# Two binary convolutions: packing in the weights instead of the activations, half of a pair at a time

## The reference

```python
def _L0_conv_ref(x, ...):           # called with _gn(x)
    xr = jnp.tile(x, (1, 4, 1, 1))                                    # 4 parallel groups
    out = bconv3x3(xr, w1, groups=4)                                  # sign(x), sign(w): 256 channels
    out = relu(batchnorm(out, bn1...))
    out = bconv3x3(out, w2, groups=4)                                 # sign(relu(.)) is 0 or 1
    out = batchnorm(out, bn2...) * repeat(lambdas, 64)
    out = out.reshape(B, 4, 64, H, W).sum(axis=1)
    return relu(out + identity)
def _L1_conv_ref(x, masks, conv_w, ...):  # called with _gn(x)
    m = resize(masks, 28 x 28); mid = x * m
    atten = sigmoid(conv7x7(concat([mean_c(mid), max_c(mid), m])))
    out = mid * atten
    rn = instance_norm(out) * in_gamma + in_beta
    return relu(5 * rn)
x = x + _L0_conv_ref(_gn(x), ...)
x = x + _L1_conv_ref(_gn(x), ...)
```

## Time and profile before

| | us |
|---|---|
| median of 3 runs (300.37 to 301.81) | 300.83 |
| profiled execution, its own time | 298.91 |
| span of that execution, first to last instruction | 297.1 |
| PE busy | 238.0 (80%) |
| DVE busy | 216.5 (73%) |
| POOL busy | 182.9 (62%) |
| ACT busy | 159.2 (54%) |
| granted TensorE clock, mean over the span | 0.918 of full |

### The profile page before, as it was taken

One profiled execution on the slowest core, in us unless ns is written; L12 is line 12 of the kernel. 1 busy time (PEld: TensorE's weight loads), 2 busy tenths in 40 slices (PEclk: granted clock), 3 DMA queues, 4 the chain that ended last, 5 costly groups with the idle time before them and its releaser, 6 DMA issues.

```text
span 297.1 us, 6991 instructions
## 1 busy us (share of the span) xinstructions
PE 238.0 (80%) x2742; PEld 152.4 (51%) x2742; DVE 216.5 (73%) x523; ACT 159.2 (54%) x191; POOL 182.9 (62%) x215
## 2 busy tenths in 40 slices
PE   8293998698998989897988798979879896866850
PEld 4262754355565556554654565456536454643640
DVE  3349642759776797989888887998696869656362
ACT  2432251275757657575758575756665774444121
POOL 2300410224534577798787969896979697967762
PEclk9668777689999999999999999999999999988775
DMA  7990000713015321632173115122512331141014
GB/s 199 307 310 14 0 2 2 182 48 110 3 57 160 114 55 58 183 97 103 58 209 113 61 61 160 57 56 85 135 54 56 119 103 57 57 160 57 0 56 162
DMA packets 11947, 28.86 MB, mean 97 GB/s; under 512 B 2286, under 2 KB 3566, under 8 KB 11758
## 3 DMA queue, kind: packets, MB, share of 16 engines
q1 hardware_dynamic: 11481, 28.13, 30.5%
q10 hardware_dynamic: 432, 0.29, 0.4%
HBM read 21.79 MB, written 6.61 MB: 96 GB/s over the span
## 4 chain that ended last, share of the span: by engine, by line
PE 56%; DVE 23%; issue 11%; DMA 3%; ACT 3%; POOL 3%; SPq 1%; POOLq 0%; DVEq 0%; ACTq 0%
PE big L901 16%; PE big L887 13%; PE big L918 10%; DVE gate L619 5%; PE small L947 5%; PE small L936 4%; DVE RD L634 4%; DVE bnst L563 4%; DMA X<-in_x 3%; DVE S L625 2%; PE small L991 2%; ACT word L471 2%; DVE red L658 2%; PE small L863 1%; POOL o L359 1%
## 5 line engine op out<-in xcount | busy, mean ns | idle before, releaser
L901 PE MATMUL big<-S,w2t 64*64 64x392 f16 x1152 | 57.3, 353 | 7.4 <-DVE S L625 7.4
L936 PE MATMUL small<-cs,o 128*112 128x130 f32 x224 | 35.1, 303 | 26.6 <-POOL o L359 19.3
L887 PE MATMUL big<-E,w1t 64*128 64x392 f16 x576 | 55.2, 334 | 0.0
L634 DVE TENSOR_SCALAR RD<-word 128x784 f16<-128x784 uint16 x32 | 33.1, 1035 | 22.2 <-ACT word L471 22.2
L901 PEld LDWEIGHTS big<-S,w2t 64*64 64x64 f16 x1152 | 33.9, 113 | 26.2 <-DVE S L625 5.1
L936 PEld LDWEIGHTS small<-cs,o 128*112 128x112 f32 x224 | 28.8, 190 | 35.7 <-POOL o L359 25.2
L359 POOL TENSOR_TENSOR o<-o,mask_b 128x784 f32<-128x784 f32 x16 | 35.6, 2226 | 15.4 <-ACT o L491 15.4
L471 ACT ACTIVATE word<-big 128x784 int32<-128x784 f32 x32 | 26.1, 815 | 27.1 <-PE big L901 27.1
L377 POOL TENSOR_TENSOR X<-X,acc 128x784 f32<-128x784 f32 x15 | 29.3, 1957 | 13.9 <-ACT acc L485 13.9
L918 PE MATMUL big<-RD,wa 128*64 128x392 f16 x384 | 36.1, 339 | 0.6 <-DVE RD L634 0.6
L887 PEld LDWEIGHTS big<-E,w1t 64*128 64x128 f16 x576 | 25.7, 95 | 21.0 <-issue 4.5
(11 more groups left out here) (118 smaller groups left out, 336.1 us busy)
## 6 DMA issues: line engine op xcount, KB each, us to landing
X<-in_x SPq DMA_DIRECT2D x16, 392.0 KB, 6.0
mask_b<-mask_rows SPq DMA_DIRECT2D x32, 196.0 KB, 3.5
out<-o SPq DMA_DIRECT2D x16, 392.0 KB, 2.4
att_b<-attention_rows SPq DMA_DIRECT2D x28, 196.0 KB, 3.7
o<-in_w SPq DMA_DIRECT2D x3, 576.0 KB, 9.1
o<-in_masks SPq DMA_DIRECT2D x1, 512.0 KB, 10.6
cs<-in_cst SPq DMA_DIRECT2D x1, 385.0 KB, 11.9
o<-in_sel SPq DMA_DIRECT2D x1, 343.0 KB
```

The lines of the kernel that those rows point to most:

```text
L634: dve.tensor_scalar(RD[:, t % 2, hh, 1, :], low2[:, hh, :], LIFT, 1.0 / UNIT, ALU.subtract, ALU.mult).then_inc(split, 1)
L887: mm = pe.matmul(acc[:, LOW + HALF * hh:LOW + HALF * (hh + 1)], w1t[64 * hh:64 * hh + 64, s, q * P:(q + 1) * P], window(RH * hh, s // 3, s ...
L901: mm = pe.matmul(acc[64 * q:64 * q + 64, LOW + HALF * r:LOW + HALF * (r + 1)], w2t[64 * r:64 * r + 64, s, 64 * q:64 * q + 64], window(RH * ...
L936: mm = pe.matmul(small[1 - n % 2][0:CP, at:at + P + 2], o[:, t, CP * j:CP * (j + 1)], cs[:, K_ID:K_ID + P + 2], start=True, stop=True)
```

## The change

What it does, by parts:

- **First convolution.** The two images of a pair are no longer joined. `sign_x` writes signs straight into `E`, image i on its own 64 partitions. Instead two channel blocks (output channels 0 to 127 and 128 to 255) are packed into one weight, 2046 times one sign plus the other. `join` and `pack_signs` go; the join matrix is used once, on the weights (`join_weights`). `conv1(t, step)` now makes 15 rows of each image in step 0 and 13 in step 1 (from the top for image 0, from the bottom for image 1), all 256 channels in words of 128 partitions.
- **Words.** `words1` and `words2` write the 32-bit words in place over the sums in PSUM. The tiles `word1`, `word2` and `gate0` are gone.
- **Gates.** ACT makes the gate of the high half by a steep sigmoid of the 16-bit half in PSUM (`high_gates`), DVE that of the low half by one comparison (`low_gates`), which waits for the former. Both write their own tile in `S`.
- **Second convolution.** Its weights are packed too (1024 times one half of the output channels plus the other), so its tiles are 64 rows by 32 columns, 8 of them, and there are 72 matmuls per half instead of 36. `high_sums` (ACT) and `low_sums` (DVE, waits for it) read the word in PSUM.
- **Mix.** Tiles of 64 by 32, four at a time, 24 matmuls per half instead of 12. Its weights are made by one DVE instruction instead of 12 on POOL.
- **PSUM.** `c1`, `c2` and `y` have one buffer each (two banks), and each half of a pair waits for the half before it to be read.
- **Order.** All four loops run over k = 1 to 22 and hold the end as well. `finish_block(k-1)` stands last in DVE's round but for `last_sum`, `relu_block` first in ACT's. The second block's steps are one round later than before. No `keep_clock` stands in the end.
- **Preparations.** w1 arrives as 128 partitions by 1152 values on ACT's DMA queue; the matrices of the 7 by 7 convolution are made on the host and loaded (`band_in`, 441 KB) instead of being made by 28 matmuls. Masks, thresholds and mix scales are as before with 6 instead of 4 columns. `repeat_picks` goes from ACT to POOL. Pairs 14 and 15 no longer send their attention through DRAM.

POOL's loop first, then ACT, DVE and PE; lines of "..." stand where lines are left out:

```diff
+            for k in range(1, STEPS):
+                if k in TERMS_AT:
+                    power1(batch(k + 1))
+                add_x(k - 2)
+                if (k - 5) % 2:
+                    attend(k - 5)
+                    scale3(k - 6)
+                    power2(k - 2)
+                else:
+                    scale3(k - 6)
+                    power2(k - 2)
+                    attend(k - 5)
+                last_sum(k - 6)
+                make_u(k - 2)
                 mask_column(k - 2)
...
+                act.activation(inside(E[:, t % 2, :]), X[:, t, :].rearrange("p (h w) -> p h w", w=W), ACT.Sign,
+                               bias=nm1[:, t:t + 1]).then_inc(signed, 1)
+
+            def words1(t, hh):
+                if has(t):
+                    act.wait_ge(conv1_done, 2 * t + hh + 1)
+                    act.activation(first_sums(hh).bitcast(I32), first_sums(hh), ACT.Copy, bias=WORD / 2,
+                                   scale=WORD / IMG).then_inc(worded1, 1)
+
+            def high_gates(t, hh):
+                if has(t):
...
+                    act.wait_ge(worded1, 2 * t + hh + 1)
+                    wait(act, conv2_done, 2 * t - 2)
+                    act.activation(gate_rows(t, hh, 0), by_rows(high_of(first_sums(hh))), ACT.Sigmoid,
+                                   bias=thr_high[:, :], scale=STEEP).then_inc(gated_high, 1)
...
+                    act.wait_ge(conv2_done, 2 * t + hh + 1)
+                    act.activation(second_sums().bitcast(I32), second_sums(), ACT.Copy, bias=LIFT,
+                                   scale=2.0 * UNIT).then_inc(worded2, 1)
+
+            def high_sums(t, hh):
+                if has(t):
+                    act.wait_ge(worded2, 2 * t + hh + 1)
+                    wait(act, y_done, 2 * t + hh - 1)
+                    act.activation(RD[:, hh, 0, :], high_of(second_sums()), ACT.Copy).then_inc(high2, 1)
...
+            act.dma_start(w1f, w1).then_inc(w1_in, 16)
...
+            for m in range(3):
+                act.activation(w1s[:, 3 * m:3 * m + 3, :].rearrange("p k o -> p (k o)"),
+                               w1f[:, 3 * m * P:3 * (m + 1) * P], ACT.Sign).then_inc(w1_signs, 1)
+            act.wait_ge(w1_joined, 3)
+            act.activation(w1t[:, 6:9, :].rearrange("p k o -> p (k o)"), y[:, 0:3 * P], ACT.Copy).then_inc(w1_ready, 1)
...
+            for k in range(1, STEPS):
+                relu_block(k - 2)
+                words1(k, 0)
+                high_gates(k, 0)
                 words2(k - 1, 1)
-                high_half(k - 1, 1)
+                high_sums(k - 1, 1)
                 sign_x(k + 1)
-                words1(k, 0)
+                last_relu(k - 6)
+                words1(k, 1)
+                high_gates(k, 1)
                 normalise2(k - 2)
-                words1(k, 1)
-                relu_block(k - 1)
-                pack_signs(k + 1)
-                last_relu(k - 5)
                 words2(k, 0)
-                high_half(k, 0)
-                sigmoid(k - 2)
```

```diff
+            def low_gates(t, hh):
...
+                    dve.wait_ge(gated_high, 2 * t + hh + 1)
+                    dve.tensor_scalar(gate_rows(t, hh, 1), by_rows(low_of(first_sums(hh))), thr_low[:, :], None,
+                                      ALU.is_gt).then_inc(gated_low, 1)
+
+            def low_sums(t, hh):
+                if has(t):
+                    dve.wait_ge(high2, 2 * t + hh + 1)
+                    dve.tensor_scalar(RD[:, hh, 1, :], low_of(second_sums()), LIFT, 1.0 / UNIT,
+                                      ALU.subtract, ALU.mult).then_inc(low2, 1)
...
+            def scale_weights(m):
+                dve.wait_ge(w1_signs, m + 2)
+                dve.tensor_tensor(w1p[:, 3 * m:3 * m + 3, :], w1s[:, 3 * m:3 * m + 3, :],
+                                  scale_s[:, :].unsqueeze(1).to_broadcast([P, 3, P]), ALU.mult).then_inc(w1_scaled, 1)
+
+            def keep_weights(m):
+                dve.wait_ge(w1_joined, m + 1)
+                dve.tensor_copy(w1t[:, 3 * m:3 * m + 3, :].rearrange("p k o -> p (k o)"),
+                                c2[:, 512 * m:512 * m + 3 * P]).then_inc(w1_ready, 1)
...
+            scales()
+            for m in range(3):
+                scale_weights(m)
+            for m in range(2):
+                keep_weights(m)
+            thresholds()
             stats_x(1)
-            sign_weights()
+            low_gates(0, 0)
             terms1(1)
+            flip_weights()
...
+            for k in range(1, STEPS):
+                if k in TERMS_AT:
...
+                attend_last(k - 5)
+                stats_o(k - 6)
...
+                low_gates(k, 0)
+                if k in TERMS_AT:
+                    make_bias1(batch(k + 1))
+                if k == 1:
+                    keep_mask_rows()
+                stats_x1(k - 2)
+                low_sums(k - 1, 1)
+                terms2(k - 2)
+                reduce_chunks(k - 3, 0)
+                reduce_chunks(k - 3, 1)
+                low_gates(k, 1)
+                reduce_chunks(k - 3, 2)
+                low_sums(k, 0)
+                finish_block(k - 1)
+                last_sum(k - 6)
```

```diff
-                wait(pe, sigm, t // 2)
+                wait(pe, y_added, t + 1)
...
+            def conv1(t, hh):
...
+                wait(pe, gated_low, 2 * t + hh)
+                wait(pe, gated_high, 2 * t + hh)
+                n = ROWS[hh] * W
                 for s in range(KS):
-                    for hh in range(2):
-                        mm = pe.matmul(acc[:, LOW + HALF * hh:LOW + HALF * (hh + 1)],
-                                       w1t[64 * hh:64 * hh + 64, s, q * P:(q + 1) * P],
-                                       window(RH * hh, s // 3, s % 3, E[64 * hh:64 * hh + 64, t % 2, :]),
+                    for i in range(2):
+                        mm = pe.matmul(c1[:, 512 - n * (1 - i):512 + n * i], w1t[64 * i:64 * i + 64, s, :],
+                                       window(START[i][hh], ROWS[hh], s, E[64 * i:64 * i + 64, t % 2, :]),
                                        start=(s == 0), stop=(s == KS - 1))
                 mm.then_inc(conv1_done, 1)
...
+                pe.wait_ge(gated_low, 2 * t + hh + 1)
+                pe.wait_ge(gated_high, 2 * t + hh + 1)
+                wait(pe, low2, 2 * t + hh)
+                wait(pe, high2, 2 * t + hh)
+                for s in range(KS):
                     for r in range(2):
-                        for q in range(2):
-                            mm = pe.matmul(acc[64 * q:64 * q + 64, LOW + HALF * r:LOW + HALF * (r + 1)],
-                                           w2t[64 * r:64 * r + 64, s, 64 * q:64 * q + 64],
-                                           window(RH * hh, s // 3, s % 3, S2[64 * r:64 * r + 64, t % 2, q, :]),
-                                           start=(s == 0), stop=(s == 8))
+                        for i in range(2):
+                            for q in range(2):
+                                at = Q32 * (2 * i + q)
+                                mm = pe.matmul(c2[at:at + Q32, LOW + HALF * r:LOW + HALF * (r + 1)],
+                                               w2t[64 * r:64 * r + 64, s, q, :],
+                                               window(RH * half_of(i, hh), RH, s, S[64 * r:64 * r + 64, t % 2, i, q, :]),
+                                               start=(s == 0), stop=(s == KS - 1))
...
+            for k in range(1, STEPS):
                 conv1(k, 0)
-                if k == 2:
+                conv2(k - 1, 1)
+                if k == 1:
+                    turn_mask()
+                mix(k - 1, 0)
+                group_2(k - 2)
+                if k == 3:
                     pe.wait_ge(mask_rows, 2)
-                group_2(k - 2)
+                turn(k - 3, 0)
+                turn(k - 3, 1)
                 conv1(k, 1)
-                if k == 1:
-                    pe.wait_ge(band_ready, 1)
-                    turn_mask()
-                    pe.wait_ge(var1, 3)
-                    band_matrices(1)
-                mix(k - 1, 0)
+                turn(k - 3, 2)
+                conv2(k, 0)
+                attention(k - 3)
                 mix(k - 1, 1)
-                join(k + 1)
-                if k == 2:
-                    pe.wait_ge(band_ready, 2)
-                for n in range(3):
-                    turn(k - 2, n)
-                conv2(k, 0)
```

More of the change, by code:

```diff
@@ L954, in keep_clock @@
                 for _ in range(n):
-                    pe.matmul(big[2][:, LOW:512], warm[:, 0:P], warm[:, :], start=True, stop=True)
+                    pe.matmul(small[0][:, 0:HALF], warm[:, 0:P], warm[:, :], start=True, stop=True)
             def spread_attention(t):
+                if not has(t) or t < POOL_ATTENDS:
+                    return
                 if t == POOL_ATTENDS:
```

618 lines of the change are left out of this document (244 added, 374 removed).

## The result

The changed kernel takes 333.99 us (median of 4 runs, 326.93 to 336.71) against 300.6 (300.13 to 301.81), ratio 1.0949 [1.0802, 1.1097]. The profile is of an execution of 336.22 us. A second set of runs of the same kernel gave 326.2 (322.80 to 329.27), ratio 1.077 [1.0682, 1.0858]. Forecast were 317.6 and a range to 334, whose upper end the first median just touches. Before spreads over 1.7 us, the changed kernel over 9.8 in the first set and 6.5 in the second, which will need a reason.

The account below looks back on a forecast made before the run. No engine was full, so waits between engines bound the round; the change would make a loop of 15.1 us. Rounds +15.1, start -4.8, end +5.0 and +1.5 gave +16.8 us: 317.6 us, with 304 to 334 holding 8 in 10.

Parts of the forecast that it names:

- start: Up to the end of `finish_block(1)`: conv1(0,0) at about 11, conv1(1,0) at 32 to 34, end at 63.0; -4.8 us.
- 13 rounds: From `finish_block(1)` to `finish_block(14)`: 13 x 15.1 + 2.1 = 198.4 against 183.3; +15.1 us.
- end: After `finish_block(14)`: last pairs go one behind the other, 51.0 against 46.0, +5.0 us, plus 1.5 for a slower clock.
- The loop: Path through the engines' ordered lists, one pair per turn: 14.7 us, 15.1 with some 14 handovers of 0.03 to 0.04.
- ACT 2.73 (2.82 forecast): First step of a round, on ACT: `relu_block`, `words1(k,0)` and `high_gates(k,0)`, 2.82 us.
- DVE 2.28 (2.28): Second step of a round, on DVE: `low_gates(k,0)`, then `stats_x1(k-2)` behind it, 2.28 us.
- PE 3.34 (3.27): Third step, on PE: `group_2(k-2)` waits for the statistics, then two turns and `conv1(k,1)`, 3.27 us.
- ACT 4.16 (4.35): Fourth step, on ACT: `words1(k,1)`, `high_gates(k,1)`, `normalise2`, `words2(k,0)` and `high_sums(k,0)`, 4.35 us.
- DVE 1.99 (1.97): Last step of a round, on DVE: `low_sums(k,0)` and `finish_block(k-1)`, 1.97 us.
- the rival of the busy time: Rounds: if statistics come in time, ACT's 11 us plus a wait of 2.0 make 13.1 per round; 292.5 us, chance 0.12.
- The rival's 330.6: Rounds: TensorE's waits for the group sum lower the clock, about 1 us more per round; 330.6 us, chance 0.26.
- the third rival: Second convolution: 32-column tiles run four at a time, 0.8 to 1.2 more per round; 328 to 333 us, chance 0.06.

Follow-up runs that it names:

- second profile: The changed kernel as it is, run once more for its spread and a second profile: 326.2 us, ratio 1.077; the profiled execution took 324.23 us.
- the one with fillers in the rounds: Changed kernel plus 9 or 16 matmuls on zeros ahead of `group_2(k-2)` on TensorE in the rounds: 315.73 us, ratio 1.051.
- the move: Changed kernel with `conv1(k,1)` put ahead of `group_2(k-2)` and the turns on TensorE: 295.94 us, ratio 0.9839.
- both moves: Changed kernel with `conv1(k,1)` ahead of `group_2` and the turns, and attention behind `mix(k-1,1)`: 297.88 us, ratio 0.9929.
- two such gains, 6 and 3 us: Attention behind the mix, added to `conv1(k,1)` first: 297.88 against 295.94 us; `scale3` first plus fillers, added to the kernel at 280.23: 280.13 us.
- one such kernel: Both reorderings on TensorE, plus pairs 14 and 15 taken together on DVE and fillers in the end, against the changed kernel: 280.23 us, ratio 0.9336.
- the two that differ from it by `scale3` and fillers in the rounds: Kernel at 280.23 us with `scale3(k-6)` ahead of `attend(k-5)` in even rounds: 280.01 us; also with 9 fillers ahead of `conv1(k,1)` there: 280.13 us.

## Why the prediction was right in direction and short in size

Terms on the span, in us, against the first profile, the second, and the one with fillers in the rounds:

| | forecast | first | second | fillers |
|---|---|---|---|---|
| start | -4.8 | -1.0 | -6.3 | -6.5 |
| 13 rounds | +15.1 | +31.9 | +25.6 | +13.6 |
| end | +6.5 | +6.0 | +6.0 | +9.3 |
| sum | +16.8 | +36.8 | +25.3 | +16.3 |

- **The loop was right, step by step.** Round 8 has ACT 2.73 (2.82 forecast), DVE 2.28 (2.28), PE 3.34 (3.27), ACT 4.16 (4.35), DVE 1.99 (1.97): 14.5 (14.7), and a round without attention takes 14.6 at full clock, so that handing over cost 0.1 and not 0.4: an instruction starts before the one ahead of it on its engine ends. What I left out was attention: its last reduction stands behind the low gates of the second half, and the mix behind attention. That is 1.0 in every second round. That these two misses cancel is luck: at full clock the 13 rounds take 196.85, 198.4 were forecast. That the statistics and the turns ahead of `conv1(k,1)` made it this long is shown by the move: rounds without attention go from 14.6 to 13.2, which is what the rival of the busy time (13.1) had priced for statistics that come in time. Its parts were others, though: in a round of 13.17 with both moves ScalarE is busy for 10.2 and waits for 3.0, where the rival had 11 and 2.0. For DVE the busy time beside the loop was too high as well (11.5, measured 9.7).
- **The term that was mis-sized is the rounds, and what was missing in it is the clock.** I forecast them at full clock and gave the fall 0.26 and 1 us per round. It came in 6 of the 13 rounds of the second profile and cost 12.0 us there, and in 11 of the first (the two without last 14.92 and 15.58), 18.3 us, 1.7 a round. The rival's 330.6 is nearer to both medians, 334.0 and 326.2, than the forecast, and its mechanism is shown by the fillers. The evidence was in hand: waits of 3 us came out of my own walk, and the earlier trace rows has the clock falling behind an idle stretch. The price was low too: the turns and the convolution behind the wait are 3 us of work, and in the round shown 1.6 were added to them.
- **The start** was right in kind, and 1.5 us better than forecast, where the clock was kind (-6.3, -6.5), though its first steps came later than thought: conv1(0,0) starts at 12.47 (11 forecast), conv1(1,0) at 37.34, and at 34.47 in the second profile (32 to 34). What made up for it there is round 2, 13.2 where I had 13.7 to 14.5; in the first profile it lasts 14.61 at a clock of 0.88.
- **The end** was right within 0.5, and pair by pair as described: `attend_last(14)` ends 32.6 behind the mark (31.3 forecast, and 1.5 added for the clock), the three last sums follow at 318.78, 324.91 and 330.16, the store takes 2.8.
- **The tiles of 32 columns** cost nothing: 72 matmuls in 1.72 us, below the 1.9 that I took. So the third rival is out.
- **Slips in the sums.** The rival of the busy time comes to 291.6 by its own terms (300.8 - 10.9 - 4.8 + 6.5), not 292.5. The range of a round, 14.2 to 15.9, leaves out the 0.3 that is said to be allowed below; with it the lower end is 13.9. Neither changes the forecast.

## What to carry to other kernels

Before counting what a change takes off an engine, walk the loop that leads through the engines' ordered lists; here DVE lost 28 us of work and each round still got longer by one at full clock. Put in that walk every instruction that stands ahead of a waited-for one, also those of other pairs (statistics ahead of a convolution, attention ahead of a mix). And where the walk shows TensorE waiting in every round, as here for 1.8 to 3.4 of 15 us, price the round at both clocks and give the lower one at least an even chance: matmuls on zeros in that wait were worth 12 to 18 us of the rounds here, and moving the next convolution ahead of it was worth more (27 us of them against the second profile). An edit that shortens the rounds in a profile need not show in the median, where the clock differs from run to run: here two such gains, 6 and 3 us, did not.

## What was not expected of the hardware

- Eight tiles of 64 rows by 32 columns run beside each other: 72 matmuls of 392 columns in 1.72 us at full clock, so they start 0.024 apart at most on average. The small matmuls of the earlier trace rows had given 0.026, and the Trainium skill (TensorE: Matmul & The Clock Gate, Wait - 56ns, not 53.3ns?) a floor of about 25 ns; the trace is a little below both.
- A one-source operation of DVE on 16-bit halves in PSUM takes 0.949 for 784 elements, against 0.51 from SBUF in the earlier trace rows. All 32 of the changed kernel lie between 0.92 and 0.98; the 32 from SBUF before lie between 0.51 and 1.89, with a median of 0.57. The trace agrees with the rule of the Trainium skill that the prediction weighed (VectorE: DVE Perf Modes, Mode 2x_2P), by which the mode that reads one source through both ports works in SBUF only.
- Writing over its own operand in PSUM cost ScalarE nothing: 0.814 for 784 elements against 0.815 into SBUF in the earlier trace rows.
- The clock's falls are not a fixed property of a program: one kernel ran its rounds at 0.90 and at 0.93, and its start at 0.77 and 0.86, in executions of the same code. What decides between them stays open. Short waits in the rounds and fillers in the end are not enough for equal times: one such kernel agreed within 0.9 us over four runs, the two that differ from it by `scale3` and fillers in the rounds spread over 8.5 and 5.3.
